# Filling the position tables of a disentangled attention layer with half-height column tiles

## The reference

```
scores = q k^T / sqrt(3 * 8)
rel    = log_bucket(i - j)                     # between -32 and 32, saturated far from the diagonal
c2p    = take(q @ pos_k^T, clip(rel + 32, 0, 63)) / sqrt(2 * 8)
p2c    = take(k @ pos_q^T, clip(-rel + 32, 0, 63)) / sqrt(2 * 8)
out    = softmax(scores + c2p + p2c^T) v
```

## Time and profile before

| | us |
|---|---|
| median of three runs | 1361.63 |
| lowest, highest | 1357.6, 1362.56 |
| the profiled execution | 1353.68 |
| its span in the trace | 1351.7 |
| mean granted clock of TensorE, of full speed | 0.886 |

### The profile page before, as it was taken

One profiled execution on the slowest core, in us unless ns is written; L12 is line 12 of the kernel. 1 busy time (PEld: TensorE's weight loads), 2 busy tenths in 40 slices (PEclk: granted clock), 3 DMA queues, 4 the chain that ended last, 5 costly groups with the idle time before them and its releaser, 6 DMA issues. The chain is left out here.

```text
span 1351.7 us, 31301 instructions
## 1 busy us (share of the span) xinstructions
PE 1049.4 (78%) x9281; PEld 883.3 (65%) x9281; DVE 955.4 (71%) x2968; ACT 682.5 (50%) x1705; POOL 548.8 (41%) x418
## 2 busy tenths in 40 slices
PE   4991331789362899999999999999999998711886
PEld 3991230688242688888788888888888886601886
DVE  6886932566571788887888888888888887530664
ACT  2444410344281566666666666666666664100443
POOL 0006317355000555554455455554545552035554
PEclk9996555899685999999999999999999999555999
DMA  5910043222259565757475665747566540052221
GB/s 142 222 41 0 1 176 129 70 79 75 68 200 266 124 154 149 166 131 171 125 172 142 148 164 138 177 121 174 141 149 159 139 109 1 0 188 94 75 78 52
DMA packets 75273, 165.91 MB, mean 123 GB/s; under 512 B 8249, under 2 KB 54784, under 8 KB 66528
## 3 DMA queue, kind: packets, MB, share of 16 engines
q1 hardware_dynamic: 69600, 152.75, 44.3%
q0 software_dynamic: 5632, 12.67, 2.7%
HBM read 130.76 MB, written 35.67 MB: 123 GB/s over the span
## 5 line engine op out<-in xcount | busy, mean ns | idle before, releaser
L1147 POOL TENSOR_SCALAR ds_scores<-ds_scores,ds_max 128x256 f32<-128x256 f32 x256 | 344.2, 1345 | 332.3 <-DVE ds_max L1366 332.2
L1358 DVE TENSOR_TENSOR ds_p2c<-ds_bank,ds_p2c 128x512 f32<-128x512 f32 x256 | 175.3, 685 | 79.7 <-PE ds_bank L1196 79.3
L1366 DVE CUSTOM_DVE_ANT_0 ds_scores<-ds_bank,ds_p2c 128x256 f32<-128x256 f32 x512 | 195.9, 419 | 0.2 <-DVE ds_p2c L1358 0.2
L1307 ACT ACTIVATE all_xt<-ds_bank 128x512 f32<-128x512 f32 x256 | 154.3, 603 | 77.6 <-PE ds_bank L1214 73.8
L1196 PE MATMUL ds_bank<-all_constants,ds_c2p_t 128*128 128x128 f32 x1024 | 159.5, 278 | 0.0
L1214 PE MATMUL ds_bank<-all_constants,ds_scores 128*128 128x128 f32 x1024 | 154.2, 272 | 1.8 <-ACT all_xt L1307 1.6
L1196 PEld LDWEIGHTS ds_bank<-all_constants,ds_c2p_t 128*128 128x128 f32 x1024 | 116.6, 141 | 35.9 <-issue 24.5
L1214 PEld LDWEIGHTS ds_bank<-all_constants,ds_scores 128*128 128x128 f32 x1024 | 119.6, 140 | 6.8 <-issue 2.2
L1187 PE MATMUL ds_bank<-ds_qr,ds_tab 64*128 64x128 f32 x1024 | 77.1, 292 | 32.5 <-DVE ds_qr L1342 28.9
L1289 ACT ACTIVATE ds_c2p_t<-ds_bank 128x256 f32<-128x256 f32 x256 | 77.8, 400 | 46.5 <-PE ds_bank L1187 46.5
L1203 PE MATMUL ds_bank<-ds_ks,ds_qs 72*128 72x256 bf16 x512 | 98.5, 273 | 2.5 <-DVE ds_max L1366 2.5
(11 more groups left out here) (253 smaller groups left out, 2138.7 us busy)
## 6 DMA issues: line engine op xcount, KB each, us to landing
ds_qr<-scratch_qk SPq DMA_DIRECT2D x32, 1024.0 KB, 10.8
ds_kr<-scratch_qk SPq DMA_DIRECT2D x32, 1024.0 KB, 13.8
ds_tab<-scratch_tables SPq DMA_DIRECT2D x64, 248.0 KB, 9.6
slots_in<-all_zero SPq DMA_DIRECT2D x2, 5160.0 KB, 39.1
ds_qs<-scratch_q_parts SPq DMA_DIRECT2D x32, 288.0 KB
ds_ks<-scratch_k_parts SPq DMA_DIRECT2D x32, 288.0 KB
0fe_xb<-slots_in SPq DMA_DIRECT2D x40, 129.0 KB
1fe_xb<-slots_in SPq DMA_DIRECT2D x40, 129.0 KB
```

The source lines that it names most:

```text
L1147: pool.tensor_scalar(S[b % NS][:, 1, :], S[b % NS][:, 1, :], mx[:, 2 * b + 1:2 * b + 2], None, ALU.subtract).then_inc(s_sub1, 1)
L1307: act.activation(PT[b], pt2[:, :].rearrange("p (k s) -> p k s", k=2), ACT.Exp).then_inc(s_exp, 1)
L1358: dve.tensor_tensor(z, pt1[b % 2][:, :].rearrange("p (a k) -> p a k", a=2), z, ALU.add).then_inc(s_z, 1)
L1366: last = dve.tensor_tensor_reduce(out=S[b % NS][:, st, :], in0=pqk[b % 2][:, st * SEQ:(st + 1) * SEQ], in1=PC[half][:, st, b, :], scale=1. ...
```

## The change

The fill of the inner groups becomes half as high. It now takes only the 64 rows of each side that lie near the diagonal. The two sides are two column tiles of 64, and both write one bank: side 0 to partitions 64 to 127, side 1 to partitions 0 to 63 (`near`). The other 64 rows of each side come from a new fill (`edge`): two bfloat16 matmuls of 64 columns of `ENDS` with `QS` or `KS`, 512 values each, again in two column tiles of one bank. ScalarE copies each of these banks in two pieces of 64 partitions. The banks of a unit remain 16; the fills become 12. Their list and `SHARE` are new: the far fill of kind 0 and quad 3 now stands in step 2, behind the near fill, that of kind 1 in step 5, and steps 6 and 7 have an edge and a far fill each.

```diff
-        RUNS = (((0, 0, 4), (1, 8, 4)), ((0, 4, 4), (1, 12, 4)), ((0, 8, 4), (1, 4, 4)))
-        FILLS = [("near", kind, runs) for kind in range(2) for runs in RUNS] + \
-                [("far", kind, (0, QUADS - 1)) for kind in range(2)] + [("far", kind, (1, 0)) for kind in range(2)]
-        FILLS = FILLS[:6] + [FILLS[6], FILLS[8], FILLS[7], FILLS[9]]
-        BANKS = [2 if f[0] == "near" else 1 for f in FILLS]
+        INNER = ((0, 8, 4), (1, 4, 4))
+        PAIRS = [[("pair", kind, grp) for grp in (0, 4)] for kind in range(2)]
+        NEAR, EDGE = ([(what, kind, None) for kind in range(2)] for what in ("near", "edge"))
+        FARS = [[("far", kind, where) for where in ((0, QUADS - 1), (1, 0))] for kind in range(2)]
+        FILLS = [PAIRS[0][0], PAIRS[0][1], NEAR[0], FARS[0][0], PAIRS[1][0], PAIRS[1][1], NEAR[1], FARS[1][0],
+                 EDGE[0], FARS[0][1], EDGE[1], FARS[1][1]]
+        BANKS = [2 if f[0] == "pair" else 1 for f in FILLS]
...
-        CONTENT_FILLS = FIRST[8]
+        CONTENT_FILLS = FIRST[FILLS.index(FARS[0][1])] + 1
...
-        SHARE = [1, 1, 1, 1, 1, 1, 2, 2]
+        SHARE = [1, 1, 2, 1, 1, 2, 2, 2]
...
-                if where[1][1] != where[0][1] + 8:
-                    for r, (side, grp, _) in enumerate(where):
-                        for a in range(4):
-                            c = TABLE - SEQ + P * side - 16 * (grp + a)
-                            last = pe.matmul(pb[r][:, a * P:(a + 1) * P], TAB[half][:, kind, c:c + P],
+                if what == "edge":
+                    pe.wait_ge(s_stack[half], 16 * 4 * (head + 1))
+                    for side, grp, _ in INNER:
+                        own = slice(side * 64, (side + 1) * 64)
+                        last = pe.matmul(pb[FIRST[n] % 2][own, :], ENDS[half][:, kind, side * FAR + own.start:side * FAR + own.stop],
+                                         (QS, KS)[kind][half][:, :].rearrange("p (b s) -> p b s", b=HALF)[:, :, grp * 16:grp * 16 + 64],
+                                         start=True, stop=True)
+                    last.then_inc(s_bm, 1)
+                    return
+                if what == "near":
+                    for a in range(4):
+                        for side, grp, _ in INNER:
+                            own = slice((1 - side) * 64, (2 - side) * 64)
+                            c = TABLE - SEQ + P * side - 16 * (grp + a) + own.start
+                            last = pe.matmul(pb[FIRST[n] % 2][own, a * P:(a + 1) * P], TAB[half][:, kind, c:c + 64],
                                              mov[:, :].rearrange("p (b g s) -> p g b s", b=HALF, s=16)[:, grp + a, :, :], start=True, stop=True)
-                        last.then_inc(s_bm, 1)
+                    last.then_inc(s_bm, 1)
                     return
...
+                if what in ("near", "edge"):
+                    act.wait_ge(s_bm, done + 1)
+                    for side, grp, count in INNER:
+                        part = side if what == "edge" else 1 - side
+                        own = slice(part * 64, (part + 1) * 64)
...
+                        last = act.activation(dst, of, ACT.Copy)
+                    last.then_inc(s_be, 1)
                     return
```

More of the change, by code:

```diff
@@ L1172, in fill @@
                     return
-                if where[1][1] != where[0][1] + 8:
-                    for r, (side, grp, _) in enumerate(where):
-                        for a in range(4):
-                            c = TABLE - SEQ + P * side - 16 * (grp + a)
-                            last = pe.matmul(pb[r][:, a * P:(a + 1) * P], TAB[half][:, kind, c:c + P],
+                if what == "edge":
[13 more added lines that the diff above has]
+                            last = pe.matmul(pb[FIRST[n] % 2][own, a * P:(a + 1) * P], TAB[half][:, kind, c:c + 64],
                                              mov[:, :].rearrange("p (b g s) -> p g b s", b=HALF, s=16)[:, grp + a, :, :], start=True, stop=True)
-                        last.then_inc(s_bm, 1)
+                    last.then_inc(s_bm, 1)
                     return
-                side, grp, _ = where[0]
                 for a in range(4):
-                    c = TABLE - SEQ + P * side - 16 * (grp + a)
+                    c = TABLE - SEQ - 16 * (where + a)
                     for tile in range(2):
                         rows = slice(tile * 64, (tile + 1) * 64)
-                        own = mov[rows, :].rearrange("p (b q g h s) -> p h q g b s", b=HALF, q=2, h=2, s=8)[:, 1 - tile, :, grp + a, :, :]
+                        own = mov[rows, :].rearrange("p (b q g h s) -> p h q g b s", b=HALF, q=2, h=2, s=8)[:, 1 - tile, :, where + a, :, :]
                         last = pe.matmul(pb[tile][:, :].rearrange("p (r a n) -> p r a n", r=2, a=4)[:, :, a, :], TAB[half][rows, kind, c:c + P],
@@ L1277, in copy @@
                     return
-                if where[1][1] != where[0][1] + 8:
-                    for r, (side, grp, count) in enumerate(where):
-                        act.wait_ge(s_bm, done + r + 1)
-                        dst = to[:, side, :, :].rearrange("p b (g s) -> p g b s", s=16)[:, grp:grp + count, :, :]
-                        act.activation(dst, pb[r][:, :].rearrange("p (g b s) -> p g b s", g=count, b=HALF), ACT.Copy).then_inc(s_be, 1)
+                if what in ("near", "edge"):
[3 more added lines that the diff above has]
+                        own = slice(part * 64, (part + 1) * 64)
+                        dst, of = to[own, side, :, grp * 16:grp * 16 + 64], pb[FIRST[n] % 2][own, :]
+                        if what == "edge":
+                            of = of.rearrange("p (b s) -> p b s", b=HALF)
+                        else:
+                            dst, of = dst.rearrange("p b (g s) -> p g b s", s=16), of.rearrange("p (g b s) -> p g b s", g=count, b=HALF)
+                        last = act.activation(dst, of, ACT.Copy)
+                    last.then_inc(s_be, 1)
                     return
@@ L1285, in copy @@
                     act.wait_ge(s_bm, done + tile + 1)
-                    at = 0
-                    for side, grp, count in where:
-                        dst = to[:, side, :, :].rearrange("p b (g h s) -> p h g b s", h=2, s=8)[:, 1 - tile, grp:grp + count, :, :]
-                        last = act.activation(dst, pb[tile][:, at * 64:(at + count) * 64].rearrange("p (g b s) -> p g b s", g=count, b=HALF), ACT.Copy)
-                        at += count
+                    for side in range(2):
+                        dst = to[:, side, :, :].rearrange("p b (g h s) -> p h g b s", h=2, s=8)[:, 1 - tile, where + 8 * side:where + 8 * side + 4, :, :]
+                        last = act.activation(dst, pb[tile][:, side * 256:(side + 1) * 256].rearrange("p (g b s) -> p g b s", g=4, b=HALF), ACT.Copy)
                     last.then_inc(s_be, 1)
```

## The result

| | before | after |
|---|---|---|
| median, us (4 runs each) | 1359.62 | 1545.34 |
| lowest, highest | 1356.81, 1362.56 | 1530.71, 1548.97 |
| span of the profiled execution | 1351.7 | 1544.5 |
| mean granted clock of TensorE | 0.886 | 0.828 |

The account below looks back on a forecast made before the run. TensorE was taken to set the pace. 30 units times 2.7 us of wait and 1.0 us of clock gave +111 us, 1465 on the profiled run and 1472 us as median forecast; the range was 1405 to 1520.

Parts of the forecast that it names:

- The mechanism: Step 2: in-order TensorE reaches the far matmul 3.7 us before its data, holding back step 3's transposes, in each unit.
- The path: Far matmul of step 2 to next load issue: 15.1 us, within a unit of 24.2 us.
- near fill of 1.09: Steps 2 and 5: the near fill in two column tiles takes 1.09 us instead of 1.89.
- start of the wait: Step 2: TensorE reaches the far matmul at 564.84, 5.4 us after the load issue.
- step 5: Term (c): near fill 1.09 instead of 1.89, a far one of 0.22, 0.2 for changing tiles; together -0.38 us.
- Rival 3: Column tiles don't pair: near fills still 1.89 us, edge pairs 0.43; +3.3 us a unit, 1491 us; chance 0.06.
- term (f): After each stop in step 2 the clock falls, slowing steps 3 and 4: 1.0 us a unit, bounds 0 and 1.75.
- The landing: The four loads of parts are complete 9.1 us after their issue (568.5), between 567.0 and 570.0.
- The sum: Per unit 2.7 us for the wait and 1.0 for the clock, over 30 units: +111 us.
- Rival 4: Deeper wait: parts land at 570.0 and the clock loses its full 1.7; 5.9 us a unit, 1539 us; chance 0.10.
- Rival 1: The clock holds because stops end before it falls: +81 us, 1442 us; chance 0.27.
- The copies (e): ScalarE: four more copies, 2.2 us a unit; bank waits of 0.5 to 1 us in steps 6 and 7, covered by VectorE's mask.

Follow-up runs that it names:

- before_far_early: The kernel before, fills unchanged in kind and size, with only both far fills of kind 0 moved to step 2: 1549.06 us, ratio 1.140.
- split_sems: The changed kernel with loads issued as QS, ENDS of kind 0, KS, ENDS of kind 1, and a semaphore for each kind: 1351.70 us, ratio 0.9938.
- busy_long: The changed kernel with 24 useless float32 matmuls put ahead of the wait in step 2: 1517.64 us, ratio 1.117.
- rows_wait: The changed kernel, but SyncE waits until the parts have landed before issuing the next unit's tables and rows: 1462.04 us, ratio 1.076.
- late_far: The changed kernel with the same twelve fills reordered so that the loaded parts are needed late, from step 5 on: 1366.12 us, ratio 1.0042.
- far_first: split_sems with each near or edge fill put behind the far one of its step: 1338.88 us, ratio 0.986.

## Why the forecast was too low

- **The mechanism** was right in kind and place: the far matmul of step 2 stands ahead of its data, in-order TensorE holds the transposes of step 3 back with it, and the load issue depends on these, so that the loss repeats in each unit. before_far_early and split_sems show it from both sides.
- **The path** of 15.1 us from far matmul to next issue (24.2 less 9.1) was right: 14.99 in the only unit of the changed kernel whose clock held, 14.97 in busy_long. With it the near fill of 1.09 (1.02 measured), the start of the wait 5.4 us after the issue (5.96 in the unit shown, 709.26 to 715.22), and step 5 were right within some half a us. Rival 3 fell: the near fill took 1.02 and not 1.89, and the two matmuls of an edge pair last 0.41 us together (728.41) where two full ones last 0.60 (575.62).
- **The clock, term (f), failed:** its size, and not its place. It was taken at 1.0 us a unit with 1.75 as its upper bound; it was 2.3 in the mean, outside its own bound. The bound came from one spell of 3.6 us at 0.53, and it was taken to lie partly within the stop. In the changed kernel (787.37) 1.4 us lay within a stop of 3.6 us, but 5.5 us of work at the low level still lay behind it, and 27 of 28 units had a fall, of 1.5 to 3.1 us. The second stretch of the earlier trace rows, 1151.06 to 1154, was cut before the clock was back. Followed further in the kernel before, both spells were some 3.4 us long, as the term assumed (0.61 over 2.94 us is 2.3 us at half, and 1.1 more follow):

```profile
452.00:455.00 3.00, 2.42 (x27) 2.04 (x28) 3.00 (x2) 1.21 (x4) 3.00 (x1) 1.00 0.96 200
...
1154.50:1155.00 0.50, 0.50 (x4) 0.50 (x4) 0.00 (x0) 0.44 (x1) 0.00 (x0) 0.50 0.00 0
...
1155.50:1156.00 0.50, 0.50 (x7) 0.50 (x7) 0.38 (x1) 0.00 (x0) 0.00 (x0) 1.00 0.00 0
```

So the rows were read rightly, but two spells elsewhere in the kernel were taken as the longest that can come. Why most spells in attend were longer stays open.
- **The landing** was taken at 9.1 us after the issue, with 10.6 as late end (570.0); it was 10.25 in the mean and 12.5 at worst. The count of packets tells when data passes, and of one unit only. rows_wait shows what it could not: with nothing behind them they land at 8.6, and the 2.5 MB behind them cost 1.6 us, unit by unit differently. Against the 9.1 taken, 10.25 is 1.15 us a unit more.
- **The sum** again, per unit: 2.7 for the wait as forecast, 1.15 for the later landing, 2.3 for the clock, and 0.1 less on the path are 6.0; from the traces it is 27.56 less 21.54 (21.60 in the mean before). The clock and the landing together are 2.45 us a unit too low, 74 us in 30 units, and the measured 186 us are 75 over the forecast. The load issues of 29 units lie 799.1 us apart after and 626.4 before, 172.7 of the 192.8 us between the spans. 5.2 more are there before the first unit's load (432.76 and 437.92), and 4.3 in that unit (44.51 us against 40.26), which was costed at nothing and has a stop of 4.97 us too. The remaining 11 us behind the last issue (1281.50) hold one more stop, of 3.65 us, with a low clock behind it, an estimated 6 us by the other units; the rest was not located.
- **The rivals.** Rival 4, a late landing with the clock's full price, came nearest (1539) with a chance of 0.10. Its two terms go together, which the chance didn't count: a later landing is a longer stop, and the kernels with longer stops had more falls. That its sum of 5.9 us a unit meets the measured 6.0 is in part luck, since it has the landing 0.35 us too late and the clock 0.6 too cheap. Rival 1, the clock holds, had 0.27 and happened in one unit. The range cut off at 1520 what the landing and the clock could make together.
- **The copies (e)** were named and sized rightly, 0.60 us each, so four more are 2.4 us a unit. In the changed kernel the waits for banks that they bring lie beside the mask, as forecast; in late_far and far_first they take back part of what the tiles save. ScalarE in step 6 of the changed kernel, the edge bank in two pieces and then the far one:

```profile
729.16 1.20 ACT L1301 ACTIVATE ds_c2p_t<-ds_bank 64x512 f32<-64x512 f32 x2
730.38 0.60 ACT L1288 ACTIVATE ds_c2p_t<-ds_bank 128x512 f32<-128x512 f32 x1
```


## What to carry to other kernels

Before an instruction that waits for a load is moved forward on an in-order engine, ask which transfers its semaphore counts, not only which data it reads: here a semaphore for each kind, with its loads issued first, turned +13.5% into -0.6%, and the order within the step made it -1.4%. A wait that recurs in each turn of a loop costs its length plus what the clock does behind it, and a landing time read from a trace in which nobody waited should be priced with the transfers that queue behind it. Smaller tiles move work to whoever empties the banks: count that engine's instructions and the free banks at each place, before the matmuls saved are counted as time.
